# Gates multiplied into the expert tiles, and gathers that add their rows to X in the transfer

## The reference

```python
x = x + 0.5 * ffn(layernorm(x))
x = x + attn(layernorm(x))
x = x + 0.5 * ffn(layernorm(x))
# ffn: 8 experts, each token uses the best 2 of them
probs = softmax(x @ Wg + bg); w, idx = top_k(probs, 2); w = w / sum(w)
comb = sum(one_hot(idx, 8) * w)
h = relu(x @ W1[e] + b1[e]);  y = h @ W2[e] + b2[e];  out = sum_e(y * comb[e])
```

## Time and profile before

| | us |
|---|---|
| median of 3 runs | 1019.24 |
| lowest and highest | 1018.61, 1019.99 |
| profiled execution: span | 1039.1 |

### The profile page before, as it was taken

One profiled execution on the slowest core, in us unless ns is written; L12 is line 12 of the kernel. 1 busy time (PEld: TensorE's weight loads), 2 busy tenths in 40 slices (PEclk: granted clock), 3 DMA queues, 4 the chain that ended last, 5 costly groups with the idle time before them and its releaser, 6 DMA issues.

```text
span 1039.1 us, 20329 instructions
## 1 busy us (share of the span) xinstructions
PE 975.9 (94%) x6512; PEld 546.9 (53%) x6512; DVE 789.0 (76%) x2255; ACT 833.7 (80%) x1194; POOL 529.3 (51%) x623
## 2 busy tenths in 40 slices
PE   7899999999999999989999999998999998888995
PEld 5687777633332488843333323332688862246673
DVE  5799999867767789857777777776878754368997
ACT  4655553599999988879999999998999988865653
POOL 5546777744444314354677766666100006555775
PEclk8999999999999999999999999999999999899998
DMA  6444223000051234420111111261444421133443
GB/s 182 165 152 133 100 102 103 14 21 20 19 147 60 75 130 163 145 89 24 36 37 35 36 37 34 57 179 36 122 139 146 143 83 49 44 127 107 131 155 121
DMA packets 59821, 96.15 MB, mean 93 GB/s; under 512 B 9179, under 2 KB 30403, under 8 KB 59715
## 3 DMA queue, kind: packets, MB, share of 16 engines
q1 hardware_dynamic: 47568, 71.50, 21.5%
q0 software_dynamic: 10752, 22.04, 7.1%
q10 hardware_dynamic: 1396, 1.31, 0.4%
HBM read 56.36 MB, written 38.45 MB: 91 GB/s over the span
## 4 chain that ended last, share of the span: by engine, by line
PE 53%; ACT 18%; issue 11%; DVE 10%; POOL 3%; DMA 3%; another core or an unknown queue 1%; SPq 0%; ACTq 0%; POOLq 0%; DVEq 0%
ACT probs L2023 10%; PE ps L1764 10%; PE ps L1749 6%; ACT sums L2023 5%; DVE low L1007 3%; PE ps L1375 3%; PE ps L1377 3%; PE ps L1376 2%; PE ps L1361 2%; PE ps L1386 2%; PE ps L1387 2%; PE ps L1391 2%; PE ps L1398 2%; PE ps L732 2%; PE ps L734 2%
## 5 line engine op out<-in xcount | busy, mean ns | idle before, releaser
L2023 ACT ACTIVATE probs<-ps 128x1024 f32<-128x1024 f32 x344 | 337.1, 1126 | 20.4 <-PE ps L1749 20.0
L1704 POOL DMA_INDIRECT found<-tiles,home x168 | 168.2, 1001 | 198.7 <-ACT sums L2023 126.9
L1692 POOL DMA_INDIRECT sorted<-xn,slot x168 | 168.1, 1000 | 179.2 <-ACT probs L2023 63.0
L1764 PE MATMUL ps<-probs,value 128*32 128x512 f32 x1376 | 185.2, 610 | 3.1 <-ACT probs L2023 1.4
L2023 ACT ACTIVATE sums<-ps 128x1024 f32<-128x1024 f32 x168 | 173.8, 1127 | 7.8 <-PE ps L1749 6.9
L1749 PE MATMUL ps<-shared 32*128 32x512 f16 x1024 | 144.7, 387 | 20.5 <-ACT probs L2023 6.8
L1188 ACT ACTIVATE high<-ps 128x512 fp32r<-128x512 f32 x176 | 101.1, 593 | 74.3 <-PE ps L734 58.7
L1007 DVE SCALAR_TENSOR_TENSOR low<-ps,high 128x512 fp32r<-128x512 f32 x176 | 113.0, 682 | 11.2 <-ACT high L1188 10.2
L1749 PEld LDWEIGHTS ps<-shared 32*128 32x128 f16 x1024 | 37.9, 91 | 157.8 <-ACT probs L2023 72.1
L1264 POOL TENSOR_TENSOR sums<-sums 128x512 f32<-128x512 f32 x59 | 76.6, 1298 | 66.6 <-DVE sums L1039 48.5
L1764 PE MATMUL ps<-sums,value 128*32 128x512 f32 x672 | 90.9, 613 | 0.2 <-ACT sums L2023 0.2
(11 more groups left out here) (202 smaller groups left out, 1869.2 us busy)
## 6 DMA issues: line engine op xcount, KB each, us to landing
found<-sorted SPq DMA_DIRECT2D x56, 256.0 KB
tiles<-sums SPq DMA_DIRECT2D x56, 256.0 KB
probs<-gates SPq DMA_DIRECT2D x24, 512.0 KB
wide<-gates SPq DMA_DIRECT2D x20, 512.0 KB
sorted<-zeros SPq DMA_DIRECT2D x16, 512.0 KB
out<-X SPq DMA_DIRECT2D x15, 256.0 KB
sorted<-xn,slot POOLq DMA_INDIRECT x168
found<-tiles,home POOLq DMA_INDIRECT x168
```

The source lines that it names most:

```text
L1692: nc.gpsimd.indirect_dma_start(sorted_rows[group_of(q)], bass.IndirectOffsetOnAxis(ap=slot[:, q % XNS, k, j:j + 1], axis=0), xn[:, rows_sl ...
L1704: nc.gpsimd.indirect_dma_start(found[:, q % 2, k, j, :], None, tile_rows[group_of(q)], bass.IndirectOffsetOnAxis(ap=home[:, q, k, j:j + 1] ...
L1764: ins = nc.tensor.matmul(ps[q * W:(q + 1) * W, MIX, :], value[:, s % 2, sd, j, m, q, :], ring[ring_at(g * UNITS + 2 * j + q // 2)][:, q % ...
L2023: nc.scalar.activation(ring[ring_at(n)], ps[:, score_banks(n), :], ACT.Exp, scale=SCORE).then_inc(sm["a_probs"], 1)
```

## The change

`send` now puts the gate into the row's last column, where the 1 was: `route_gates` writes the gate of the first expert into `xn`, four sends follow, GpSimd waits until these have landed, overwrites the column with the gate of the second expert, and issues the other four. Before the slot of `xn` is used again for another job, GpSimd sets the column back to 1 (`renew_last_column`). A tile that has been loaded hands its column of gates to a small buffer (`keep_gates`), the row of gates is left out when the turned tile is copied (the row of ones stays in `xh`), and `copy_out` multiplies by the gate where it only copied. `collect` gathers with `compute_op=ALU.add` straight into X; the second four gathers of a job wait on GpSimd until its first four have landed. The steps in which sends and gathers are issued change, and `route_gates` moves one head group earlier. What VectorE and ScalarE did to combine the gathered rows is gone. Loads of tiles no longer wait for a combination.

```diff
-LAST_SENDS = 2, 4, 6, 8, 10, 12, 14, 16
+SENDS, RUSH_SENDS = (4, 5, 6, 8, 10, 12, 14, 15), (4, 5, 6, 7, 8, 9, 10, 11)
+GATHERS, RUSH_GATHERS = (0, 1, 2, 3, 7, 9, 11, 13), (0, 1, 2, 3, 12, 13, 14, 15)
-COMBINED = {(14, 2): 0, (15, 0): 1, (15, 2): 2, (15, 3): 3}
-ADDED = {(0, 3): 8, (0, 4): 9, ... (3, 3): 20, (3, 4): 21}
...
 def load_tile(t):
-                    reached(sp, sm["c_added"], GROUP[y] - 1)
-                if tile_at(t) == 2:
-                    reached(sp, sm["c_added"], GROUP[y])
                 reached(sp, sm["t_turned"], t - 3)
+                reached(sp, sm["t_gate"], t - 3)
...
 def early_gpsimd(pool, n, e):
+            if e == 4 and early_at(n) is not None:
+                renew_last_column(pool, early_at(n))
...
 def route_gates(dve, q):
-            nc.vector.tensor_scalar(gates[:, q, 0, :], rinv[:, :], 0.5, None, ALU.mult)
-            nc.vector.scalar_tensor_tensor(gates[:, q, 1, :], second[:, u, :], 0.5, rinv[:, :], ALU.mult, ALU.mult)
+            dve.wait_ge(sm["r_turned"], q + 1)
+            nc.vector.tensor_scalar(xn[:, rows_slot(q), :, D - 1], rinv[:, :], 0.5, None, ALU.mult)
+            reached(dve, sm["r_exchanged"], q - 1)
+            nc.vector.scalar_tensor_tensor(second_gate[:, u, :], second[:, u, :], 0.5, rinv[:, :], ALU.mult, ALU.mult)
...
-        def combine_half(dve, q, k): ...
-        def scale_half(act, q, k): ...
-        def add_half(dve, q, k): ...
...
 def vector_stream(dve, a, b, before_slot):
+            def keep_gates(t):
+                dve.wait_ge(tile_in[tile_slot(t)], 16 * loads_of_slot(t))
+                rows = tile_rows_in[:, tile_slot(t), :].rearrange("p (j d) -> p j d", d=D)
+                nc.vector.tensor_copy(tile_gate[:, t % HELD, :], rows[:, :, D - 1])
-                nc.vector.tensor_copy(tile_out[:, t % 2, :], ps[:, TILE_BACK, :])
+                nc.vector.tensor_tensor(tile_out[:, t % 2, :]..., ps[:, TILE_BACK, :]...,
+                                        tile_gate[:, t % HELD, :].unsqueeze(2).to_broadcast([P, J, D]), ALU.mult)
...
+        def renew_last_column(pool, q):
+            other = before_in_slot(q)
+            if other is not None:
+                pool.wait_ge(sent[other % XNS], 16 * TOPK * J * (other // XNS + 1))
+                nc.gpsimd.memset(xn[:, rows_slot(q), :, D - 1:D], 1.0)
...
 def send(pool, q, n):
+            if n == J:
+                pool.wait_ge(sent[q % XNS], 16 * (TOPK * J * (q // XNS) + J))
+                pool.wait_ge(sm["r_gates"], q + 1)
+                nc.gpsimd.tensor_copy(xn[:, rows_slot(q), :, D - 1], second_gate[:, q % 2, :])
+                pool.wait_ge(sm["r_exchanged"], q + 1)
...
 def collect(pool, q, n):
-                reached(pool, sm["c_added"], q - 1)
+            if n == J:
+                pool.wait_ge(gathered[q % 2], 16 * (TOPK * J * (q // 2) + J))
-            nc.gpsimd.indirect_dma_start(found[:, q % 2, k, j, :], None, tile_rows[group_of(q)],
-                                         bass.IndirectOffsetOnAxis(ap=home[:, q, k, j:j + 1], axis=0))
+            nc.gpsimd.indirect_dma_start(tokens(sorted_seq(q), j, 1), None, tile_rows[group_of(q)],
+                                         bass.IndirectOffsetOnAxis(ap=home[:, q, k, j:j + 1], axis=0),
+                                         compute_op=ALU.add)
...
 def attn_gpsimd(pool, s, half):     # steps i of sequence s; RUSH = (4, 13)
-                if s == RUSH[0]:
-                    if half == 0:
-                        pool.wait_ge(sm["a_probs"], first + LAST_SENDS[i])
-                        send(pool, earlier, i)
+                sends, gathers = (RUSH_SENDS, RUSH_GATHERS) if s in RUSH else (SENDS, GATHERS)
+                if earlier is not None and i in sends:
+                    paced(i)
+                    send(pool, earlier, sends.index(i))
+                if 0 <= q < NJOBS[0] and i in gathers:
+                    paced(i)
+                    collect(pool, q, gathers.index(i))
```

More of the change, by code:

```diff
@@ L226, in before_in_slot, with renewed @@
     return max([k for k in range(q) if rows_slot(k) == rows_slot(q)], default=None)
+def renewed(q):
+    return len([k for k in range(q + 1) if before_in_slot(k) is not None])
 def third(m):
@@ L304, in build @@
         rinv = sb("rinv", [P, J])
-        gates = sb("gates_sorted", [P, SORTED, TOPK, J])
+        second_gate = sb("second_gate", [P, 2, J])
+        tile_gate = sb("tile_gate", [P, HELD, J])
         zrowf = sb("zrowf", [P, E])
@@ L455, in tiles_stored, with added @@
             eng.wait_ge(tile_stored[1], 16 * (t // 2))
+        def added(eng, q):
+            eng.wait_ge(gathered[q % 2], 16 * TOPK * J * (q // 2 + 1))
         @block.sync
@@ L787, in early_scalar @@
                 q = early_at(n)
-                other = before_in_slot(q)
-                if other is not None:
-                    act.wait_ge(sent[other % XNS], 16 * TOPK * J * (other // XNS + 1))
+                if before_in_slot(q) is not None:
+                    act.wait_ge(sm["r_renewed"], renewed(q))
                 norm_rows_scaled(act, "r_", sorted_seq(q), q, route_place(q), q % 2,
@@ L1308, in route_rows @@
         def route_rows(dve, q):
-            other = before_in_slot(q)
-            if other is not None:
-                dve.wait_ge(sent[other % XNS], 16 * TOPK * J * (other // XNS + 1))
+            if before_in_slot(q) is not None:
+                dve.wait_ge(sm["r_renewed"], renewed(q))
             norm_rows(dve, "r_", sorted_seq(q), q, route_place(q), q % 2, lambda rows, u, j: (xn[:, rows_slot(q), j, 0:D - 1], rows[:, 0:D - 1]),
@@ L1625, in vector_stream @@
                 if in_stream(i + 2, a, b):
+                    keep_gates(i + 2)
                     x_low(i + 2)
@@ L1989, in attn_vector @@
                     route_copy_rows(dve, job)
-                if hg == 1 and earlier is not None:
+                if hg == 0 and earlier is not None:
                     route_gates(dve, earlier)
@@ L2076, in attn_gpsimd @@
                     norm_pool(pool, "r_", job, route_place(job))
+                    renew_last_column(pool, job)
                 if i == 7 and more:
@@ L2085, in attn_gpsimd @@
                     norm_pool(pool, "r_", extra, route_place(extra))
+                    renew_last_column(pool, extra)
                 if s == S - 1 and i == 10:
                     norm_pool(pool, "f_", WHOLE + 2, place(WHOLE + 2))
-                if s == RUSH[0]:
-                    if half == 0:
-                        pool.wait_ge(sm["a_probs"], first + LAST_SENDS[i])
-                        send(pool, earlier, i)
-                elif earlier is not None and (i % 2 == 0 if s < RUSH[1] else i in (0, 2, 4, 6, 8, 10, 12, 13)):
+                sends, gathers = (RUSH_SENDS, RUSH_GATHERS) if s in RUSH else (SENDS, GATHERS)
+                if earlier is not None and i in sends:
                     paced(i)
-                    send(pool, earlier, (i + 1) // 2)
-                if q == 0 and i in (0, 1, 2, 3, 5, 7, 9, 11):
+                    send(pool, earlier, sends.index(i))
+                if 0 <= q < NJOBS[0] and i in gathers:
                     paced(i)
-                    collect(pool, 0, i if i < 4 else i // 2 + 2)
-                if 0 < q < NJOBS[0] and i % 2 == 1 and i < 12:
-                    paced(i)
-                    collect(pool, q, i // 2 + 2)
-                if 0 <= q < NJOBS[0] - 1 and i in (13, 15):
-                    paced(i)
-                    collect(pool, q + 1, i // 2 - 6)
+                    collect(pool, q, gathers.index(i))
                 if s in COLLECTED:
@@ L2231, in first_stream @@
                     route_slots(dve, extra_at(i, 5))
-                if extra_at(i, 6) is not None:
-                    route_gates(dve, extra_at(i, 6))
+                if extra_at(i, 5) is not None:
+                    route_gates(dve, extra_at(i, 5))
                 if extra_at(i, 0) is not None:
```

96 lines of the change are left out of this document (31 added, 65 removed).

## The result

The changed kernel takes 1104.92 us (median of 4 runs, 1103.97 to 1106.41), the kernel before 1019.62 in the same comparison. The ratio is 1.0831, with a 95% interval of 1.0814 to 1.0848. I had forecast 1028, in a range up to 1046. The sign was right, the size was not. One execution of a later run took 1405.81 us at a granted clock of 0.59; it is left out of that run's median and ratio.

What follows compares the result with a forecast made beforehand. TensorE was taken to bound the tile streams, ScalarE attention, GpSimd second bound of the last stage. Terms -2.4 + 0.5 + 7.0 - 0.5 + 3.9 = +8.5 us gave a median near 1028, range 1015 to 1046.

Steps and rivals of the forecast that it cites:

- What a gather costs: All gathers: an adding gather costs the same as a plain one, 969 ns at the median; upper bound 1493 ns.
- The first rival: Everywhere: adding transfers are dearer to issue, GpSimd becomes the bound; up to 24 us more, result near 1052; chance 0.22.
- Combination gone in attention: Stage 4: nine jobs lose eight short VectorE instructions each; eight periods at 0.3 us give -2.4 us, bounds 0 and -7.
- Sequence 4 and the first stream: Late sends delay the first tile's load, TensorE stalls and loses clock: +7.0 us; gate copies in the first stream: +0.5.
- Sequence 13 and the second stream: Ahead of the second stream: sends bunched before the last four gathers go out earlier; -0.5 us, bounds -1 and +3.
- Last stage: Last stage: GpSimd's waits less slack +9.1, earlier chain start -2, last store -3.2; sum +3.9 us, lower bound -3.1.
- six waits: Last stage, GpSimd, after 954.49: one landing wait per job, 3 x 0.3 + 1.4 + 2 x 4.9 = 12.1 us.
- The end: End of the last stage: the last store no longer waits for the scaling and the addition, -3.2 us.
- The rival in which VectorE bounds the last stage: Last stage: GpSimd's waits stay below its slack, 14 additions go, at least -12.7 us, time 1011; chance 0.12.
- The rival in which only the first stream is late: Last stage even or slightly better with quiet landings, -3.1 instead of +3.9: 1021, or 1018 with smaller stall; chance 0.18.

Runs made afterwards that it cites:

- the long execution: Profile of the unchanged kernel that the prediction used: span 1039.1 us, against a median of 1019.24 us in its unprofiled runs.
- the second profile: The kernel before, run again without a change to get another profile: 1020.09 us, ratio 1.0003, span 1017.9 us.
- The last experiment on it: Changed kernel, ScalarE setting the column back in stage 1, sequence 4's sends in steps 3 to 8 behind the attention's norm: 1096.13 us, ratio 1.0762.

## Why the prediction was wrong

**The step that failed** is "What a gather costs": "I take the lower, as the rows are as many and as long". It was worth nothing in the sum and is +60 us (added alone) to about +64 us (taken away alone) on the chip. The first rival ("adding transfers are dearer to issue", 0.22) is what happened. Its price, 24 us at up to 1493 ns, was too low for three reasons. The surcharge is 0.59 us, so above its upper bound of 0.52, which came from the longest plain gather: a plain form cannot bound another form from above. It counted 46 gathers of the last chain, but the stage held 62, and 11 more came into it because stage 6 was full before it ended: in the changed kernel 24 gathers start in it, 1.84 us apart where they follow each other directly, and before it was 34 at 1.25 us. And stage 4 was left out: eight adding gathers there cost a period 1.4 us, and 10 us (with the change) to 16 us (added alone) in all.

**What the rest of the sum was worth** is read from the run with plain gathers, whose span is 18.8 us above that of before, where my sum without the gathers was +8.5.

- Combination gone in attention: -2.4 forecast, +0.2 measured in stage 4. The difference of periods that I used was in the long execution only. (It was also misread: from exponential to exponential, sequences 1 to 3 take 29.7 us in it, not 30.0.) In the second profile the period is 29.9 with the combination, with plain gathers and no combination it is 29.8 to 29.9, and there was nothing to gain.
- Sequence 4 and the first stream: +7.5 forecast (7.0 and 0.5), 3.5 + 2.4 = 5.9 measured. The mechanism was right step for step: the late sends, the turn waiting for its load (4.8 us forecast, 4.35 measured in the changed kernel), the low clock behind it (0.50 for 3.4 us, then 0.65 for 4). The last experiment on it gave the time back by order alone.
- Sequence 13 and the second stream: -0.5 forecast. The turn waits 1.36 us for its load with plain gathers and 2.12 us in the second profile of before, so -0.8. In the profile that I forecast from, it did not wait at all (no idle time before 731.28); that the load was the bound there was a misreading that came right in the other profile.
- Stage 1: not priced; the waits for sends seemed to take the place of one that ScalarE had the earlier trace rows. Now GpSimd waits, and its sums of the whole sequences queue behind it. It is 4.2 us in this run. Behind the first whole sequence it is 4.4 us in the changed kernel, and 0.6 to 0.8 where ScalarE sets its own column. In the changed kernel:

```profile
123.54 0.11 POOL L1664 MEMSET xn<- 128x4 f32 x1 [3.48 <-DMA sorted<-xn,slot]
```

- Last stage: +3.9 forecast, +8.4 measured. I had 12.1 us for six waits; with plain gathers the trace has 16.7 for all in the stage. In the changed kernel there are nine, since I had counted from the first sum only. Two of them fall on a broadcast of the gates, as forecast. One takes 4.09 us where I had 4.9, and the DMA engines' share is 1.01 in the window ahead of it. The other, ahead of the stretch that I counted, takes 7.31 us. The other seven take 0.7 to 2.1 us.

```profile
942.41 1.54 POOL L1695 DMA_INDIRECT X<-tiles,home  x1 [7.31 <-DMA X<-tiles,home]
...
956.00:960.00 4.00, 0.10 (x1) 0.00 (x0) 0.00 (x0) 0.69 (x2) 2.81 (x2) 1.00 1.01 340
```

  The end saved most of what it should: the last store follows the last gather by 3.3 us (1096.21 to 1099.49), against 5.9, so 2.6 us where I had 3.2.
- The rival in which VectorE bounds the last stage had a real core: in the second profile VectorE is busy 102 of the last 116 us. But its gain is 4.7 us, and only without any wait. The rival in which only the first stream is late needed quiet landings in the last stage; two of nine were not.

The Trainium skill, in Collectives: The Full Stack, The bandwidth ceiling, has an adding transfer of a collective read two sources with two read descriptors for a chunk, where a copy has one. This bore on the rival that held. The traces here count packets, not descriptors, and show more than twice as many: the queue of GpSimd's DMAs went from 10752 packets to 29568 for the same bytes, so from 32 to 144 for each gather. The busy share of the 16 engines by this queue only rose from 7.2% to 11.2%.

```profile
q0 software_dynamic: 10752, 22.04, 7.2%
...
q0 software_dynamic: 29568, 22.04, 11.2%
```

By the Trainium skill, DMA: Bandwidth & Descriptors, Anatomy of one DMA, a landing would be 2.15 us, an estimate from its 2.0 us plus 64 KB at 436 GB/s. Plain gathers here land in 2.6 us at the median, adding ones in 3.4, and up to 9.3; the measurement decides.

## What to carry to other kernels

A change that takes work from two engines and gives it to the queue of a third is judged by the third: count its instructions in every stage at the price of the new form, with the backlog that one stage hands to the next. Where that form is in no trace, the plain form does not bound it from above, and one short run that measures it is worth more than the rest of the sum. And before small terms are taken from one profiled execution, see whether its span agrees with the median; 20 us of surplus sat in just those stages here. When two stages of the same code differ, look at the granted clock in them and cut them again behind the difference.

## What the runs showed of the hardware

- An indirect gather of 128 rows of 512 bytes that adds keeps GpSimd 1.55 us where a plain one takes 0.97, in HBM-to-SBUF gathers into X or into a buffer alike. At 32 rows it is 1.35 against 0.88. It splits into 144 packets, not 32, and lands in 3.4 us at the median, not 2.6. Issued at 929.88, ahead of a window in which the DMA engines are full (share 1.05 in 934 to 938), it took 9.3.
- The next ordinary instruction of GpSimd is recorded from 0.98 us after the start of an adding gather, while the gather is recorded to 1.54: such records overlap, and their sum is more than the time.
- The clock that TensorE is granted in the first whole sequence differs from one execution to the next. In 16 to 46 us it was 0.83, 0.84, 0.88, 0.90, 0.97 and 0.97 in six profiles, and the second sequence began at 46.9, 46.1, 45.5, 44.4, 43.1 and 42.8 us, in the same order.
- What stays open: what GpSimd does in the extra 0.6 us. It hardly depends on the rows; no run here looks inside the instruction. Why the clock of the first sequence differs is open too.
